# The maxima's rows issued from ScalarE's queue, a loop of 120 steps and another order at the beginning, in an attention block on one core

## The reference

```
q = (route @ wq + bq).reshape(b_, r_, k_, H, D)
k = (route @ wk + bk).reshape(b_, r_, k_, H, D)
v = (route @ wv + bv).reshape(b_, r_, k_, H, D)
scores = jnp.einsum('brkhd,brnhd->brknh', q, k) / D ** 0.5
attn = jax.nn.softmax(scores, axis=3)
out = jnp.einsum('brknh,brnhd->brkhd', attn, v).reshape(b_, r_, k_, m_)
out = out @ wo + bo
x = _layernorm(route + out, ln1_g, ln1_b)
ff = jax.nn.relu(x @ w1 + b1) @ w2 + b2
return _layernorm(x + ff, ln2_g, ln2_b)
```

## Time and profile before

| | |
|---|---|
| median of 3 runs | 4289.76 us |
| the profiled execution, its time | 4295.68 us |
| the profiled execution, span of its trace | 4293.6 us |
| PE busy | 4178.0 us, 97% |
| DVE busy | 3694.2 us, 86% |
| POOL busy | 3616.9 us, 84% |
| ACT busy | 3424.5 us, 80% |
| mean granted clock of TensorE | 0.994 of 2.4 GHz |

### The profile page before, as it was taken

How to read it: one execution, slowest core, us unless ns; L and a number is a source line. 1 busy time by engine, 2 the same in 40 slices (tenths; PEclk the granted TensorE clock), 3 DMA queues, 4 the chain that set the end, 5 groups by cost and what they waited for, 6 DMA issues and landing times.

```text
span 4293.6 us, 151787 instructions
## 1 busy us (share of the span) xinstructions
PE 4178.0 (97%) x50954; PEld 3638.6 (85%) x50954; DVE 3694.2 (86%) x9739; ACT 3424.5 (80%) x5889; POOL 3616.9 (84%) x4620
## 2 busy tenths in 40 slices
PE   5999999999999999999999999999999999999998
PEld 4888888888888888888888888888888888888886
DVE  5888888888888888888888888888888888888886
ACT  3888887878888887888888877888887888888886
POOL 4888888888888888888888888888888888888887
PEclk8999999999999999999999999999999999999999
DMA  5555655555656565555555555555565556555562
GB/s 124 145 148 146 154 144 149 146 141 147 153 141 154 145 152 145 145 148 150 148 146 152 147 141 148 144 149 151 144 155 138 149 145 155 146 150 148 146 154 59
DMA packets 1294636, 621.92 MB, mean 145 GB/s; under 512 B 636544, under 2 KB 1293696, under 8 KB 1293824
## 3 DMA queue, kind: packets, MB, share of 16 engines
q1 hardware_dynamic: 1024016, 477.81, 45.7%
q10 hardware_dynamic: 269808, 133.99, 10.7%
HBM read 135.40 MB, written 67.11 MB: 47 GB/s over the span
## 4 chain that ended last, share of the span: by engine, by line
PE 77%; SPq 9%; issue 5%; DMA 3%; DVE 3%; ACT 2%; POOL 2%; ACTq 0%; DVEq 0%; POOLq 0%
PE s_ps L681 10%; PE oT_ps L708 10%; PE bankB L667 10%; PE bankC L646 9%; PE bankC L667 9%; PE sT_ps L695 9%; SPq L246 7%; PE bankB L646 7%; PE bankA L721 5%; PE bankA L771 4%; DMA stack<-parts 3%; PE bankA L646 3%; PE bankB L640 2%; SPq L240 2%; PE oT_ps L764 1%
## 5 line engine op out<-in xcount | busy, mean ns | idle before, releaser
L398 ACT ACTIVATE prob_sb<-sT_ps 128x1024 f32<-128x1024 f32 x1024 | 1044.2, 1020 | 610.9 <-PE sT_ps L695 595.1
L511 DVE TENSOR_REDUCE max_sb<-s_ps 128x8 f32<-128x1024 f32 x1024 | 1213.2, 1185 | 17.0 <-PE s_ps L681 14.6
L271 POOL TENSOR_TENSOR parts<-rest_sb,parts 128x512 bf16<-128x512 f32 x512 | 585.8, 1166 | 223.5 <-ACT parts L372 223.5
L681 PEld LDWEIGHTS s_ps<-stack 96*128 96x128 bf16 x8192 | 463.8, 98 | 307.9 <-issue 243.3
L681 PE MATMUL s_ps<-stack 96*128 96x128 bf16 x8192 | 639.6, 221 | 54.3 <-DMA stack<-parts 25.7
L695 PE MATMUL sT_ps<-stack 99*128 99x128 bf16 x8192 | 629.0, 219 | 1.3 <-ACT prob_sb L398 1.3
L708 PE MATMUL oT_ps<-prob_sb,v_ones 128*32 128x128 f32 x16384 | 553.6, 276 | 3.0 <-ACT prob_sb L398 2.2
L667 PE MATMUL bankB<-w_sb,h_sb 128*128 128x128 f32 x4096 | 525.4, 281 | 7.3 <-ACT h_sb L379 6.6
L708 PEld LDWEIGHTS oT_ps<-prob_sb,v_ones 128*32 128x32 f32 x16384 | 416.3, 109 | 128.2 <-DVE max_parts L609 69.2
L695 PEld LDWEIGHTS sT_ps<-stack 99*128 99x128 bf16 x8192 | 504.3, 98 | 3.0 <-ACT prob_sb L398 1.8
L667 PE MATMUL bankC<-w_sb,h_sb 128*128 128x128 f32 x4096 | 499.2, 275 | 0.0
(11 more groups left out here) (78 smaller groups left out, 8721.1 us busy)
## 6 DMA issues: line engine op xcount, KB each, us to landing
stack<-parts SPq DMA_DIRECT2D x3072, 128.0 KB, 2.6
x_blocks<-in_x SPq DMA_DIRECT2D x1024, 64.0 KB, 2.1
out<-out_sb ACTq DMA_DIRECT2D x256, 256.0 KB, 3.5
x_sb<-in_x ACTq DMA_DIRECT2D x255, 256.0 KB, 3.1
stack<-max_parts SPq DMA_DIRECT2D x768, 8.0 KB, 3.1
w_sb<-in_L_conv_w SPq DMA_DIRECT2D x2, 256.0 KB, 3.0
x_sb<-in_x SPq DMA_DIRECT2D x1, 256.0 KB, 3.1
be_row<-in_L_conv_ln_b SPq DMA_DIRECT2D x2, 64.0 KB, 5.3
```

The source lines that it names most:

```text
L271: pool.tensor_tensor(parts[:, r % 2, 3 * c + LO], rest_sb[:, c], parts[:, r % 2, 3 * c + MID], ALU.subtract).then_inc(lo_split, 1)
L398: act.activation(prob_sb[:, s % 2], sT_ps[:], ACT.Exp, scale=float(D) ** -0.5).then_inc(exp_done, 1)
L511: dve.reduce_max(max_sb[:, (r - lag) % 2, :, s], s_ps[:].rearrange("p (h k) -> p h k", h=H), AX.X).then_inc(max_done, 1)
L681: ins = pe.matmul(s_ps[:, h * P:(h + 1) * P], stack[0:PROD, (r - lag) % 4, 0, h, tok], stack[0:PROD, (r - lag) % 4, 1, h, tok], start=True ...
```

## The change

The three transfers of the maxima's rows leave SP's step and go to ACT's. There the wait for `max_parts_made` and the first of them stand behind the first relu, the second behind the second relu, and the third behind the copy of the values. The load of x moves behind the first `apply2`, and the store of an output moves from the end of ACT's step at lag 7 to a place behind the third and fourth relu of the next step (lag 8). UNROLL becomes 120 and LEAD 12, so the loop runs twice and jumps back once, and the written-out tail begins at step 252. At the beginning ACT calls an activation on a constant first and then issues the 16 loads of `wo_sb` and `bv_col` which SP issued before; the rows of ones are written as pairs of bf16 through float32 (4096 elements per row instead of 8192), half of them by DVE at the start and half by POOL before step 0; DVE transposes the first x before it splits the weights.

```diff
+TWO_ONES = float(np.array([0x3F803F80], np.uint32).view(np.float32)[0])
-UNROLL = 48
-LEAD = 8
+UNROLL = 120
+LEAD = 12
...
         @block.sync
...
-            for h in range(H):
-                at = (h % HU) * VW + (h // HU) * D
-                sp.dma_start(wo_sb[at:at + D], wo[h * D:(h + 1) * D]).then_inc(consts_loaded, DMA)
-                sp.dma_start(bv_col[at:at + D], col(bv[h * D:(h + 1) * D]),
-                             allow_slow_non_contiguous=True).then_inc(consts_loaded, DMA)
...
-                if live(t, r, 2):
-                    sp.wait_ge(max_parts_made, upto(t, r, 2, plus=1))
-                    for part in range(MAXROWS):
-                        sp.dma_start(stack[PROD + part:PROD + part + 1, (r - 2) % 4, 0],
-                                     max_parts[:, part]).then_inc(max_rows_loaded, DMA)
...
         @block.gpsimd
...
-            pool.memset(v_ones[:], 1.0).then_inc(consts_set, 1)
             pool.memset(minus_half[:], -0.5).then_inc(consts_set, 1)
             pool.memset(minus_one[:], -1.0).then_inc(consts_set, 1)
             pool.memset(eps_sb[:], EPS).then_inc(consts_set, 1)
-            pool.wait_ge(consts_set, N_SET)
-            pool.memset(stack[PROD:PROD + MAXROWS, 0:2, 1], 1.0).then_inc(stack_ones_set, 1)
+            pool.memset(v_ones[:], 1.0).then_inc(v_ones_set, 1)
+            pool.wait_ge(v_ones_set, 1)
+            pool.memset(stack[PROD:PROD + MAXROWS, 2:4, 1].bitcast(F32), TWO_ONES).then_inc(stack_ones_set, 1)
...
-            pool.wait_ge(lo_split, 2)
-            pool.memset(stack[PROD:PROD + MAXROWS, 2:4, 1], 1.0).then_inc(stack_ones_set, 1)
-            pool.wait_ge(stack_ones_set, 2)
...
         @block.scalar
         def _(act):
-            act.wait_ge(qk_loaded, N_QK * DMA)
+            act.wait_ge(consts_set, N_SET)
+            act.activation(pause_act[:], minus_one[:, 0:1], ACT.Exp)
+
+            for h in range(H):
+                at = (h % HU) * VW + (h // HU) * D
+                act.dma_start(wo_sb[at:at + D], wo[h * D:(h + 1) * D]).then_inc(consts_loaded, DMA)
+                act.dma_start(bv_col[at:at + D], col(bv[h * D:(h + 1) * D]),
+                             allow_slow_non_contiguous=True).then_inc(consts_loaded, DMA)
...
+            def max_row(t, r, part):
+
+                act.dma_start(stack[PROD + part:PROD + part + 1, (r - 2) % 4, 0],
+                              max_parts[:, part]).then_inc(max_rows_loaded, DMA)
...
                     relu(t, r, 6, 3)
+                if live(t, r, 8):
+                    act.wait_ge(out_ready, upto(t, r, 8, plus=1))
+                    act.dma_start(out_g[t + (r - 8)], out_sb[:, (r - 8) % 2]).then_inc(out_stored[(r - 8) % 2], DMA)
...
                     relu(t, r, 5, 0)
+                if live(t, r, 2):
+                    act.wait_ge(max_parts_made, upto(t, r, 2, plus=1))
+                    max_row(t, r, HI)
+                if live(t, r, 5):
                     relu(t, r, 5, 1)
+                if live(t, r, 2):
+                    max_row(t, r, MID)
...
+                if live(t, r, 2):
+                    max_row(t, r, LO)
+                if live(t, r, 6):
+                    apply2(t, r, 6, 0)
                 if live(t, r, -1):
...
-                if live(t, r, 7):
-                    act.wait_ge(out_ready, upto(t, r, 7, plus=1))
-                    act.dma_start(out_g[t + (r - 7)], out_sb[:, (r - 7) % 2]).then_inc(out_stored[(r - 7) % 2], DMA)
-                if live(t, r, 6):
-                    apply2(t, r, 6, 0)
...
-            iterate(act, step, 1, LEAD, LAST, 7)
+            iterate(act, step, 1, LEAD, LAST, 8)

         @block.vector
         def _(dve):
+            dve.memset(stack[PROD:PROD + MAXROWS, 0:2, 1].bitcast(F32), TWO_ONES).then_inc(stack_ones_set, 1)
...
+            turn_x(0, 0)
             dve.wait_ge(qk_loaded, N_QK * DMA)
```

More of the change, by code:

```diff
@@ L25 @@
+import numpy as np
 import concourse.bass as bass
@@ L84, in build @@
         minus_half, minus_one, eps_sb = (sb(n, [P, SEQS]) for n in ("minus_half", "minus_one", "eps_sb"))
-        pause = sb("pause", [P, 1])
+        pause, pause_act = sb("pause", [P, 1]), sb("pause_act", [P, 1])
         x_sb = sb("x_sb", [P, 2, SEQS, P])
@@ L117, in build @@
         ident_zero, ident_set, consts_set = sem("ident_zero"), sem("ident_set"), sem("consts_set")
-        stack_ones_set = sem("stack_ones_set")
+        stack_ones_set, v_ones_set = sem("stack_ones_set"), sem("v_ones_set")
         bv_wide_set, w_products_done, consts_made = sem("bv_wide_set"), sem("w_products_done"), sem("consts_made")
@@ L190, in iterate, with col @@
                 step(0, r)
-        N_QK, N_CONST, N_SET, N_MADE = 5, 11 + 2 * H, 4, 4
+        N_QK, N_CONST, N_SET, N_MADE = 5, 11 + 2 * H, 3, 4
         block = ctx.enter_context(nc.Block())
+        def col(v):
+            return v.rearrange("(p a) -> p a", a=1)
         @block.sync
@@ L346, in step @@
                     lo_part(t, r, 1)
[L348 removed]
+            pool.wait_ge(stack_ones_set, 2)
             step(0, 0)
[L350 to L352 removed]
             pool.wait_ge(consts_loaded, N_CONST * DMA)
@@ L452, in step @@
                     act.dma_start(x_sb[:, (r + 1) % 2], x_g[t + (r + 1)]).then_inc(x_loaded[(r + 1) % 2], DMA)
-                if live(t, r, 7):
-                    act.wait_ge(out_ready, upto(t, r, 7, plus=1))
-                    act.dma_start(out_g[t + (r - 7)], out_sb[:, (r - 7) % 2]).then_inc(out_stored[(r - 7) % 2], DMA)
-                if live(t, r, 6):
-                    apply2(t, r, 6, 0)
-            act.wait_ge(consts_set, N_SET)
+            act.wait_ge(qk_loaded, N_QK * DMA)
+            act.wait_ge(v_ones_set, 1)
             step(0, 0)
@@ L462, in _, with turn_x @@
             act.wait_ge(consts_made, N_MADE)
-            iterate(act, step, 1, LEAD, LAST, 7)
+            iterate(act, step, 1, LEAD, LAST, 8)
         @block.vector
         def _(dve):
+            dve.memset(stack[PROD:PROD + MAXROWS, 0:2, 1].bitcast(F32), TWO_ONES).then_inc(stack_ones_set, 1)
+            def turn_x(t, r):
+                dve.wait_ge(blocks_loaded[r % 2], upto_dma(t, r, 0, per=P // BLK * DMA))
+                if (v := upto(t, r, 0)) is not None:
+                    dve.wait_ge(v_done, v)
+                if (v := upto(t, r, 0)) is not None:
+                    dve.wait_ge(xT_lo, v)
+                dve.transpose(xT_sb[:], x_blocks[:, r % 2]).then_inc(x_turned, 1)
+            turn_x(0, 0)
             dve.wait_ge(qk_loaded, N_QK * DMA)
@@ L562, in step @@
                 row_max(t, r, 1)
-                if live(t, r, 0):
-                    dve.wait_ge(blocks_loaded[r % 2], upto_dma(t, r, 0, per=P // BLK * DMA))
-                    if (v := upto(t, r, 0)) is not None:
-                        dve.wait_ge(v_done, v)
-                    if (v := upto(t, r, 0)) is not None:
-                        dve.wait_ge(xT_lo, v)
-                    dve.transpose(xT_sb[:], x_blocks[:, r % 2]).then_inc(x_turned, 1)
+                if live(t, r, 0) and (r > 0 or not isinstance(t, int)):
+                    turn_x(t, r)
                 if live(t, r, 6):
@@ L792, in _ @@
             pe.wait_ge(stack_ones_set, 2)
+            pe.wait_ge(v_ones_set, 1)
             iterate(pe, step, 1, LEAD, LAST, 6)
```

3 lines of the change are left out of this document (removed).

## The result

The changed kernel took 4273.85 us in the median of 8 runs, the kernel before 4289.02 beside it: a ratio of 0.9968, with a 95% interval of 0.9957 to 0.9979. The forecast was 4231, with a range of 4212 to 4266. It is faster, by 0.2 to 0.4%, but by 15 us where 59 were forecast, and the time lies above the range.

A forecast was written before the change was run, and what follows sets the result against it. PE's own work was taken as the bound, its standstills as winnable: 20.5 (loop) + 25 (SP's queue) + 13.3 (beginning) = 58.8 us, ACT's queue, load and store 0; 4289.76 - 58.8 = 4231 us, range 4212 to 4266.

The forecast's parts named there:

- What bounds the kernel: Whole kernel: PE's own work is the bound, a regular step stays 16.15 us, only PE's standstills (67.5 us) can be won.
- The loop: Steady loop: one jump back instead of four removes 20.5 us, bounds 18.2 and 22.6.
- Rival B: Loop: the jump costs as much in all, or longer code brings gaps; the 20.5 go, 4251 us; chance 0.08.
- The beginning: Start and pipeline filling: earlier constants, loads and transposition, and shorter waits for parts, gain 13.3 us, bounds 10.5 and 17.
- SP's queue: Steady steps: without the maxima's rows SP starts the parts 1.1 us earlier; 25 us removed, bounds 0 and 38.
- Load and store: ACT's steady step: load slips 1.5 us behind `apply2`, store goes to 2013.7 or so; cost 0.
- ACT's queue: ACT's steady step: one added wait and three issues, covered by relus and value copy; cost 0, bounds 0 and 24 us.
- A: Steady steps: load and store beside the parts lengthen the 12 issues, margin given back; 4256 us, 4248 to 4262; chance 0.21.
- C: Every step: ACT's second transfer waits 0.6 us for SP's first parts, values late for projection; 88 us slower, 4319; chance 0.05.
- The rule of descriptor generation: SP and ACT issuing together: a queue locks the one generator, so ACT's second and third transfers would wait behind SP's parts.

The follow-up runs named there:

- cover_clear: The changed kernel with row transfers behind the first and second exponentials, load behind the third, store behind the two high parts: 4231.65 us, ratio 0.9854.
- ldst_only: The changed kernel with the maxima's rows back on SP's queue ahead of the parts, load and store at their new places: 4281.24 us, ratio 0.9984.
- loop_and_start: The changed kernel with its steady part put back (rows on SP's queue, load and store at their old places): 4259.38 us, ratio 0.9922.
- small_store: The changed kernel with each group's store writing only 16 of its 128 partitions: 4262.48 us, ratio 0.9934.
- load_cover: The changed kernel with the load alone moved, from behind `apply2` to behind the third exponential: 4250.94 us, ratio 0.9903.
- ldst_cover: The changed kernel with the store behind the four normalisations and the load behind the third exponential, rows left in place: 4259.21 us, ratio 0.9914.
- clear_only: The changed kernel with the load behind the third exponential and the store behind the two high parts, rows left in place: 4249.11 us, ratio 0.9896.

## Why the prediction failed, point by point

- **What bounds the kernel: right.** A regular step is 16.15 us before and after, and with every loss taken away (`cover_clear`) it is 16.14.
- **The loop, 20.5: right.** Four jumps of 26.7 us became one of 7.0, 19.7 less; one step of 23.18 us. Rival B is out.
- **The beginning, 13.3 with bounds 10.5 and 17: 10.2, just below.** The two large terms held. PE's first matmul is at 11.55 us, 12.6 forecast; L802 (then L787) at 20.17, 20.6 forecast. Up to there 11.3 us are gained, where 10.8 were forecast. The term that failed is the last, 2.5 for the waits for parts during the filling: they are 3.5 us where the earlier trace rows has 4.2. Besides, 1.9 of the 11.3 us are gone again when PE first transposes maxima (43.56 against 52.93, 9.4 earlier); why is open.
- **SP's queue, 25: mis-sized to 13.4.** The first half of the step held, to the hundredth: the parts start 1.19 us behind L262. "The margin before PE's scores grows from 0.4 to 1.5 us, less what the load and the store, now issued beside the parts, may add" was left with the "may" at nothing. It was the whole margin: with load and store beside them the last part lands 1.1 us later after its issue begins (3.63 against 2.52), and the 12 issues take 0.4 longer. With nothing beside the parts it has landed 11.73 us behind the low part's start instead of 12.95 (`cover_clear`), and the term is worth what was forecast or more: 34.7 us in the gaps. The reading that 12.1 us were spread over some 200 steps at a few hundredths was wrong too: 11.9 of them lie in 56 steps of 0.05 to 0.5 us.
- **Load and store, 0: wrong, 24 us.** These are the same microseconds as in the terms above and below, 14 of SP's and 10 of ACT's. "The load slips by 1.5 us ... and is wanted a step later" looked at who wants the load, and not at what the load takes from others while it runs. By the step's own times the load would be issued at about 2011.0, 1.3 us into the parts' issues; that could be read from the rows. The sentence that the two no longer following each other speaks for fewer slow issues was wrong in its result: with the rows on SP the new places cost 25 us more before the scores (`ldst_only`).
- **ACT's queue, 0, bounds 0 and 24: 21.1 us, near the upper bound** (24.5 against the trace of `loop_and_start`). This is the largest term that failed. The cover was counted with the median issue, 0.60, against covers of 0.68, 0.69 and 0.60. That holds in a regular step. But the step of the earlier trace rows has issues of 0.90 and more, and a slow issue on ACT delays ACT. The same stalls were counted as a gain on SP's side and left out on the side to which the transfers moved. Some 8 of the 21.1 hang on the load behind `apply2` as well: they go when the load is moved (29.1 to 21.0 in the two gaps).
- **The rivals.** A (4256) had its mechanism right: the margin gained is given back by load and store. It too held ACT's cost for at most 4 us and so came out 18 us low. C foresaw the place, the value copy late for the projection, but as a delay of 0.6 us in each step; it came in 45 steps and cost 12.7 us. Its cause, SP's first issues, is not seen: in the slow step above the second row, issued at 2021.41 across SP's start at 2021.61, took 0.52, and that is the median of all steps.
- **The rule of descriptor generation.** SP's 12 issues take 8.60 us before the change, in most steps with none of ACT's among them, 8.63 in `small_store`, with four of ACT's among them, 8.62 in `load_cover`, with three and a whole store, and 8.98 in the changed kernel, with the four and both large transfers whole. So the number of issues on the other queue costs next to nothing, and only the two large transfers together lengthen the train, by 0.4 us. The Trainium skill's rule ("Perfetto Trace Analysis", "DMA Instruction — HWDGE (DVE, Sync)") tells of the DVE and Sync sequencers and not of ScalarE's; for SP and ACT nothing of its size is seen here, and C's 88 us did not come.

## What the runs showed of the hardware

**Slow issues and instruction packets fall together.** The transfers in windows of 2.8 us in the kernel before show it: first the slow issues of the earlier trace rows (706.70 to 709.50), then the same place a step earlier, where the issues were quick (columns: queue and kind, packets, MB, share of 16 engines).

```profile
q10 hardware_dynamic: 441, 0.22, 27.4%
q8 instruction: 1, 0.02, 3.0%
q1 hardware_dynamic: 51, 0.01, 2.0%
```

```profile
q10 hardware_dynamic: 161, 0.08, 10.1%
q1 hardware_dynamic: 96, 0.02, 3.6%
```

3.0% of 16 engines over 2.8 us is one engine busy for 1.3 us, about as long as the stall. In the two slow steps of the changed kernel shown above such a packet starts at 2021.75 and at 2225.81, just before the slow issue (2022.04 and 2225.89).

Over the steady steps of the kernel before, all 77 issues of a row that lasted over 0.84 us overlap a packet of this queue, q8, and none of 539 without a packet lasted so long; but 107 that overlap one were quick. By steps, with a window of 3 us from the first row's issue on, in the changed kernel: of 103 steps in which a packet starts 98 have an issue on ACT's queue of over 0.7 us, of 137 without one 4; the mean steps are 16.48 and 16.25 us. In the kernel before 115 steps with a packet lost 34.6 us and 122 without 6.2. The packets of the other instruction queue, q14, show nothing of the kind (before: 7 of 27 steps with one have a slow issue, 77 of 210 without). On SP's queue the large transfers are a second cause: 139 slow issues of parts in the changed kernel overlap no packet, 3 in the kernel before and 12 in `small_store`.

q8 moves 417 packets of 16 KB, 6.83 MB or 1.6 a step, in the changed kernel and in each kernel here with its loop, and 423 in the kernel before. The Trainium skill ("Runtime: NRT & Kernel Launch", "Instruction fetch mechanics") says that instructions arrive in blocks of 16 KiB and that crossing a boundary is "mostly hidden". The size agrees with the trace (1 packet, 0.02 MB); hidden it was only where nobody was waiting for an issue. That the packet causes the stall is inferred from coincidence in time and from these counts. No run took the packets away, so it isn't shown further than that. `cover_clear` has the packets too and loses 5.1 us outside its jump: what can be chosen is what stands behind an issue.

**A large transfer beside the parts delays them.** One 256 KB load, issued 1.27 us (median) behind the first of a train of twelve 128 KB transfers between places in SBUF, raised their median landing from 2.8 to 3.5 us (`load_cover` against the changed kernel), and PE's losses at the parts from 3.8 to 17.8. The page's median landing does not foretell the loss, though. `small_store`, which lost 8.4 us, and `ldst_cover`, which lost 15.0, have:

```profile
stack<-parts SPq DMA_DIRECT2D x3072, 128.0 KB, 3.4
```

```profile
stack<-parts SPq DMA_DIRECT2D x3072, 128.0 KB, 2.6
```

What PE waits for is the last of the twelve. Counted from the low part's start to its landing (medians of 240 steps), the last part takes 12.96 us in the changed kernel, 12.71 in `ldst_cover`, 12.56 in `small_store`, 12.37 in `load_cover` and 11.83 in `clear_only`, and the losses before the scores stand in the same order: 17.8, 15.0, 8.4, 3.8 and below 2 us.

## What to carry over

Cost an issue on a busy engine by its slow form and not by its median, and put it behind an operation that outlasts it or ahead of idle time; if stalls are counted as a gain on the queue that gets lighter, count them as a cost on the one that gets the transfers. When a transfer moves in time, ask what is in flight where it arrives: here the queue position of three small rows was worth 33 us, the place of one large load took 24 back and the cover of the rows on ACT 15 to 18 more, so that the steady part of the change lost. Splitting the lost time by the gap on the bounding engine, before and after, shows such gains and losses side by side where the total shows almost nothing.
